# First edge pass: GpSimd waits for three of the four gathers ahead, between source and target rows and between groups

## The reference, cut to what matters

```python
src, dst = edge_index[0], edge_index[1]
msg_s = (s_n @ Ws_src)[src] + (s_n @ Ws_dst)[dst]
msg_v = einsum('ncx,cd->ndx', v_n, Wv_src)[src] + einsum('ncx,cd->ndx', v_n, Wv_dst)[dst]
w1 = rbf @ W_rbf
m1_s, m1_v = _cg_tp(msg_s, msg_v, y0, y1, w1[...])       # products with the edge's harmonics
a = leaky(m1_s @ W_alpha) . alpha_dot                     # attention logits
val_s, val_v = m1_s @ Ws_val, m1_v @ Wv_val * sigmoid(val_s @ Wg)
m2_s, m2_v = _cg_tp(sigmoid(val_s), val_v, y0, y1, w2...)
h = [m2_s @ Ws_vlin, m2_v @ Wv_vlin]                      # summed later by target, weighted by softmax
```

## Time and profile before

| | us |
|---|---|
| median of 3 runs | 10209.57 |
| lowest and highest | 10196.67 and 10226.99 |
| the profiled execution | 10306.75 |
| its span, first to last instruction | 10304.9 |
| busy in the span: PE, PEld, DVE, ACT, POOL | 8085.0, 6348.5, 6778.5, 5206.1, 5020.8 |

### The profile page before, as it was taken

The page is one execution under the profiler, slowest core; times in us unless marked ns, Lnnn a source line. Parts: engine busy times, 40 slices in busy tenths (PEclk is TensorE's granted clock), DMA queues, the critical chain, the costliest instruction groups (busy, mean ns, idle before and its releaser), DMA issues. The chain is left out here.

```text
span 10304.9 us, 195656 instructions
## 1 busy us (share of the span) xinstructions
PE 8085.0 (78%) x43972; PEld 6348.5 (62%) x43973; DVE 6778.5 (66%) x16742; ACT 5206.1 (51%) x16950; POOL 5020.8 (49%) x5222
## 2 busy tenths in 40 slices
PE   5788888888878878878888869988777777666667
PEld 3677776777767767767777759964444443333335
DVE  7666666666666666666666778877666555555445
ACT  5545555555545444455555541157665555554444
POOL 1545555555545555455555529715444444444441
PEclk7777777777777777777777879999888888888888
DMA  7323222222222222222222228664333333333225
GB/s 231 75 71 76 76 74 74 75 76 77 76 71 76 74 73 73 71 74 76 76 74 75 77 63 250 212 125 107 95 93 92 90 89 88 86 84 83 80 80 168
DMA packets 971866, 967.97 MB, mean 94 GB/s; under 512 B 452750, under 2 KB 788750, under 8 KB 971662
## 3 DMA queue, kind: packets, MB, share of 16 engines
q0 software_dynamic: 225792, 385.65, 15.3%
q1 hardware_dynamic: 512032, 346.40, 12.2%
q10 hardware_dynamic: 233936, 234.90, 6.8%
HBM read 677.57 MB, written 288.65 MB: 94 GB/s over the span
## 5 line engine op out<-in xcount | busy, mean ns | idle before, releaser
L745 POOL DMA_INDIRECT e_g_dst<-table_dst,e_idx x1568 | 1494.0, 953 | 1791.9 <-ACT logits L898 1421.9
L2015 POOL DMA_INDIRECT f_e<-table,f_src x1568 | 1495.0, 953 | 1658.6 <-DVE f_dot L2171 830.1
L784 PE MATMUL e_ps_t<-ident,e_m 128*128 128x128 f32 (+1 forms) x7840 | 1537.8, 343 | 748.6 <-issue 425.4
L745 POOL DMA_INDIRECT e_g_src<-table_src,e_idx x1568 | 1497.2, 955 | 1015.0 <-issue 675.6
L784 PEld LDWEIGHTS e_ps_t<-ident,e_m 128*128 128x128 f32 (+1 forms) x7840 | 1177.6, 176 | 948.9 <-issue 647.5
L2070 PE MATMUL f_ps_a<-sums 128*128 128x384 f32 x3936 | 1697.7, 583 | 5.8 <-DVE sums L2170 3.4
L2070 PEld LDWEIGHTS f_ps_a<-sums 128*128 128x128 f32 x3936 | 852.9, 228 | 676.1 <-issue 395.4
L2059 PE MATMUL f_ps_w<-f_w,f_hidden 64*128 64x192 f32 x3936 | 539.5, 400 | 834.2 <-issue 421.1
L2170 DVE TENSOR_TENSOR f_ey<-f_e,f_ps_w 128x384 f32<-128x384 f32 x492 | 272.6, 554 | 1349.3 <-POOLq L1998 1170.0
L877 ACT ACTIVATE e_m1t<-e_ps_t 128x512 f32<-128x512 f32 (+1 forms) x1176 | 684.3, 598 | 899.0 <-remote 359.9
L2059 PEld LDWEIGHTS f_ps_w<-f_w,f_hidden 64*128 64x128 f32 x3936 | 367.1, 217 | 919.0 <-issue 464.1
(11 more groups left out here) (268 smaller groups left out, 18215.4 us busy)
## 6 DMA issues: line engine op xcount, KB each, us to landing
edge_values<-e_h ACTq DMA_DIRECT2D x392, 330.0 KB
r_h<-edge_values SPq DMA_DIRECT2D x196, 660.0 KB, 4.0
sums<-sums ACTq DMA_DIRECT2D x492, 192.0 KB
e_g_src<-table_src,e_idx POOLq DMA_INDIRECT x1568
e_g_dst<-table_dst,e_idx POOLq DMA_INDIRECT x1568
f_e<-table,f_src POOLq DMA_INDIRECT x1568
f_rbf<-basis SPq DMA_DIRECT2D x492, 48.0 KB
basis<-t_part SPq DMA_DIRECT2D x42, 448.0 KB, 3.1
```

Source lines behind the costliest of these rows:

```text
L745: pool.indirect_dma_start(out=into[:, r, t, :], out_offset=None, in_=table, in_offset=bass.IndirectOffsetOnAxis(ap=idx[:, r, c:c + 1], axi ...
L784: last = nc.tensor.transpose(ps_t[bank][0:channels, t * P:(t + 1) * P], rows(t), ident[:])
L2015: pool.indirect_dma_start(out=rows_of_units[:, (place * RING + r) * T + t, :], out_offset=None, in_=table, in_offset=bass.IndirectOffsetOn ...
```

## The change

The semaphore `gathered[r]` is split in three for each slot: `from_src[r]` counts tiles 0 to 2 of the source rows (48 a group), `from_dst[r]` tiles 0 to 2 of the target rows (48), `fourths[r]` the fourth tile of both (32). GpSimd gets two waits more in each group:

- before the first source gather of a group it waits until three of the four target gathers of the group before have landed;
- before the first target gather it waits until three of the four source gathers of the same group have landed.

SP and DVE, which waited for one semaphore, now wait for three with the same meaning: all eight gathers have landed. No gather, transfer or computation is added, taken out or changed.

```diff
-        idx_in, y_in, rbf_in, gathered = ([sem(f"{n}{r}") for r in range(RING)]
-                                          for n in ("idx_in", "y_in", "rbf_in", "gathered"))
+        idx_in, y_in, rbf_in, from_src, from_dst, fourths = ([sem(f"{n}{r}") for r in range(RING)]
+                                          for n in ("idx_in", "y_in", "rbf_in", "from_src", "from_dst", "fourths"))
...
-                    wait(sp, gathered[r], i * 32 * T)
+                    wait(sp, from_src[r], i * 16 * (T - 1))
+                    sp.sem_inc(issued, 1)
+                    wait(sp, from_dst[r], i * 16 * (T - 1))
+                    sp.sem_inc(issued, 1)
+                    wait(sp, fourths[r], i * 32)
...
+                if not isinstance(u, int) or u > 0:
+                    pool.wait_ge(from_dst[(r - 1) % RING], (i + 1 if r else i) * 16 * (T - 1))
                 pool.sem_inc(issued, 1)
-                for side, (table, into) in enumerate(((table_src, g_src), (table_dst, g_dst))):
+                for side, (table, into, landed) in enumerate(((table_src, g_src, from_src),
+                                                              (table_dst, g_dst, from_dst))):
                     if side == 1 and (not isinstance(u, int) or u >= RING):
                         wait(pool, gated, u - RING)
+                    if side == 1:
+                        pool.wait_ge(from_src[r], (i + 1) * 16 * (T - 1))
                         pool.sem_inc(issued, 1)
...
-                        ).then_inc(gathered[r], 16)
+                        ).then_inc(landed[r] if t < T - 1 else fourths[r], 16)
...
-                dve.wait_ge(gathered[r], (i + 1) * 32 * T)
+                dve.wait_ge(from_src[r], (i + 1) * 16 * (T - 1))
+                dve.wait_ge(from_dst[r], (i + 1) * 16 * (T - 1))
+                dve.wait_ge(fourths[r], (i + 1) * 32)
```

## The result

The changed kernel takes 9881.79 us, the median of 3 runs (9875.61 to 9894.07), against 10209.57: a ratio of 0.968, with an interval from 0.965 to 0.971. That is 328 us less, where 135 were forecast. The direction and the mechanism held; two terms of the sum were too small. 9882 us lies outside the 9990 to 10140 that the prediction gave as the range of its likeliest case, and nearer to the 9800 of its rival "stronger" than to its own 10075.

A forecast was written before the change was run, and what follows sets the result against it. It took the bound to be a chain of message, source burst, PE's release and gate, with POOL's gap deciding. The terms -46 + 30 - 119 = -135 us took 10209.6 to about 10075 us, range 9850 to 10290.

The forecast's parts named there:

- the mechanism: PE's results are held while POOL issues gathers, passing about 1.2 us after a burst if POOL pauses that long.
- stronger: Rival: gaps a tenth of a microsecond beyond 1.0 suffice, all 29 long groups go: 9800 us, chance 0.15.
- nothing: Rival: POOL is off the path, the gap only a sign of a late message: 10210 to 10240 us, chance 0.18.
- slower: Rival: the burst's end sets the gate, the wider gap opens nothing, lateness is paid: 10340 us, chance 0.22.
- (a): Wider gap before source bursts: 43% of the 179 short gaps open, DVE's `e_partial` no longer waits there: -46 us.
- `e_partial` under 400 us: Sign of being right: DVE's `e_partial` waits for a remote release under 400 us instead of 529.
- The threshold of 1.25 us: POOL's gap before a source burst: over about 1.25 us, PE's results pass.
- the price of waking up from a landing: From a gather's landing to POOL's next gather: taken as 0.9 us, within bounds of 0.8 to 0.95.
- (b): Source bursts of groups whose gap was wide already move back a little: +30 us.
- (c): Long groups of 24.4 us: the landing wait cures two thirds of 19 with short target-to-source gaps: -119 us.
- The waits taken at nothing: DVE's and SP's three waits for one: at most a tenth of a microsecond a group, taken as 0.
- To carry that difference over: The profiled execution lies 97 us over the median; the difference was kept unchanged in forecasting about 10075 us.

The follow-up runs named there:

- e4: Kernel before, with four more semaphore increments on POOL ahead of each source burst (0.31 us of delay) and no landing wait; ratio 0.989.
- e10: Changed kernel, with POOL's landing waits after the first two gathers of a burst in place of three; ratio 0.985.
- e9: Kernel before, unaltered, run again on another chip; ratio 0.999.
- e5: Changed kernel, unaltered, run again on another chip; ratio 0.970 to the kernel before.
- e3: Kernel before, with only the semaphore split in three and three waits on DVE and SP, no landing wait on POOL; ratio 0.992.
- e16: Changed kernel, unaltered, run again on a fourth chip; ratio 0.971 to the kernel before.
- e1: Changed kernel without the wait between source and target rows, so only the wait between groups; ratio 0.987 to the kernel before.
- e2: Changed kernel without the wait between groups, so only the wait between source and target rows; ratio 0.987 to the kernel before.
- e17: Changed kernel, with four semaphore increments (0.31 us) behind the message wait in place of the wait between groups; ratio 0.980 to the kernel before.
- e12: Kernel before, with 28 semaphore increments on POOL ahead of each of the message and gate waits, no landing wait; ratio 0.984.
- e11: Changed kernel, with POOL's landing waits after all four gathers of a burst in place of three; ratio 0.992 to the kernel before.
- e6: Kernel before, with 4 semaphore increments on POOL ahead of the message wait and 10 ahead of the gate wait; ratio 1.010.
- e7: Kernel before, with 12 semaphore increments on POOL ahead of the third source gather; ratio 1.004.
- e8: Changed kernel, with four semaphore increments on POOL ahead of the message wait; ratio 0.977 to the kernel before.

## Why the prediction was right in its mechanism, and where its size was wrong

**The mechanism was right.** PE's results were late because POOL's source burst began too soon, and the change cures that by starting it later. e4 shows it with a delay alone, e10 with a wait that never delays. The rival "nothing" fell with the 208 held groups of all 378 that became 31 (228 and 78 in e9 and e5), "slower" with the sign. The prediction's sentence that all 179 short gaps were followed by a late `e_partial` leaves something out: 21 more gaps of 0.99 or 1.00 us have the pause of 1.88 us inside the burst, and none of them was held. That speaks for the mechanism, since there PE's results passed while POOL paused. The Trainium skill, "SBUF — State Buffer", section "SBUF: two separate sides", would have made (a) 0; POOL's start moves `e_partial` by some 3.5 us in e4 (6.8 to 3.3 at the medians of held and early open groups), and so something of PE's way depends on it. Whether that is a port or PE's release of semaphores, no run here tells; a fetch of instructions it is not, as far as the trace records them (e3).

**What it would show.** Gaps spread from 1.1 to 2 us: yes, 21 of 378 are left at 0.9 to 1.02. `e_partial` under 400 us: 99. Fewer than 15 groups over 20 us: one on the first chip, 16 and 12 on the others. POOL's waits name gathers: yes.

**Term (a), the step that failed.** The share of short gaps that open was put at 43 to 45%; of the early bursts 95% were open in the first result, 74 and 67% in e5 and e16. The threshold of 1.25 us was a little high: the switch lies between 1.1 and 1.4 (6.6 to 6.9 us after the gate), and in the first result at its lower end. More wrong was the price of waking up from a landing: "from 0.8 to 0.95 are its bounds, and I take 0.9", and it is 1.13. The bounds came from a release by an engine, the nearest row, but of another kind. With the same landings of the kernel before, 1.13 opens 78% at a threshold of 1.2 us and 68% at 1.25, where 0.9 gives 43 and 41%; the 95% of the first result takes 1.13 and a threshold of 1.1 (94%). (a) and (b) together were to bring 16 us. The groups of up to 17 us brought 0.50 x 353 = some 176 us between the first two kernels, and 154 us between e9 and e5. With 95% open the prediction's own sum gives (0.95 x 13.5 + 0.05 x 28.0) / (0.95 + 0.10) = 13.55 and so 149 - 30 = 119 us. The rest is not accounted for; the higher clock, which the sum left out, is a candidate.

**Term (b)** is within that sum and can't be told apart.

**Term (c), the second one too small.** Forecast 119 us, by curing two thirds of 19 groups. The excess fell by 216 us, and by 151 between e9 and e5. That a wait for a landing cures long groups was right. Wrong was the gap on which the term was counted, the one from target to source rows ("the landing wait lifts these gaps to about 1.0"), which the wait between groups lifts. e1 has that wait alone and no such gap under 0.7 us, and keeps 28 groups over 20 us and 303 us of excess; e2 has the wait within a group alone and 124 such gaps, and 115 us. What it takes first is the other gap, from source to target rows; e17 shows that the first one counts beside it. So it was wrong, too, to count only the 19 groups with a short gap ahead of the source burst. The 10 with 1.0 us ahead of it went too. They have no gap of 0.30 on either side, but a target burst 0.75 to 0.87 us behind the source burst, which the wait within a group lifts to 1.05 or more as well. Most of what is left of the excess is a loss not foreseen: 20 to 26 groups of 17 to 20 us, where there were 4 or 5. The second rule weighed, from "Runtime: NRT & Kernel Launch", section "Instruction fetch mechanics", in the Trainium skill, made (c) 0 by putting the long groups down to the loop's branch. In e12 the pause stands in 32 rounds and no group is over 23 us, so it isn't that by itself; and no packet of instructions stands in the pass (e3), so what makes the pause is open.

**The rival "stronger".** Its two conditions came close to true in the first result: 95% of the early bursts open, 28 of 29 groups over 20 us gone. It had a chance of 0.15. It says 9800 us and not 9882 because it took the long groups' whole excess as gained, where groups of 17 to 20 us took part of it back. On the other two chips, with 67 to 74% open and 12 to 16 groups over 20 us, the gain lies between it and the forecast.

**The sum by its own steps:** 176 + 216 = 392 us by the tally, 394 by the two traces. The medians differ by 328, since the profiled execution of the kernel before lay 97 us above its median, that of the changed kernel at its own. To carry that difference over "as it is" was wrong too: in the changed kernel it wasn't there.

**The waits taken at nothing** (DVE's and SP's) may not be nothing: e3, which has them and the split alone, gains 0.8%. How much of the 328 us that is can't be said, and it isn't explained. And the prediction added its terms up, while the two waits together bring 0.012 more than their sum over e3 (e5).

**The clock** stands at 0.77 in the pass of the kernel before and e9, 0.81 in the changed kernel, 0.80 in e5 and e4, 0.77 in e11. What it follows isn't shown: e11 has no held group and the low value, e4 the high one with 26 groups of over 23 us. How much of a group's 1.1 us it gives back wasn't tried; PE's busy time a group is 0.54 us less, which is the most that faster matmuls can have given.

## What to carry to other kernels

A producer that runs three groups ahead can still set the pace, by when it starts and not by how much it does: look for two alternating lengths of a group, and measure the start of its bursts against the event that both chains hang on. Two waits that each bring 1.3% may cure two different things, so tally each kind of group and not only the time. Before two halves are added up, take off what both contain: here the split of the semaphores, 0.8 of the 1.3%. And price a wait by a release of its own kind: a DMA landing woke GpSimd 0.3 us later than an engine's release did.

## What the runs showed that I had not expected

- From the landing of a gather to the start of the next on GpSimd: 1.13 us (1.09 to 1.20). From a release by VectorE or ScalarE: 0.81 to 0.84.
- Four semaphore increments behind a late wait cost 0.31 us; ten to twelve of them ahead of a wait or between two gathers cost GpSimd nothing that its timeline shows, since its queue runs ahead under the 0.95 us of a gather. Yet the three kernels with such increments were 0.4 to 1% slower than their neighbours without (e6, e7, e8).
- The time at which a source burst starts, between 6.5 and 6.9 us after the gate, decides whether TensorE's next result comes some 2.4 to 4.3 us (the middle half in the changed kernel) or 6.8 us after the message.
- The pause of 1.88 us inside a burst came and went (32 rounds or 1) with semaphores that only other engines wait for, with no instruction packet in the pass. A burst with the pause held no `e_partial` back, though it began as early as those that did.
- All 29 long groups of the kernel before stand behind a target burst that began less than 1 us after a source burst, and of the 341 groups without that none is over 16.5 us.
